# A decoder layer on one core: two groups overlapped in the opening, own rows for groups 2 and 3, 71 tiles, fewer idle products

## The reference

```python
x = x + self_attention(layernorm(x))             # 16 heads of 8, RoPE on q and k
x = x + cross_attention(layernorm(x), context)   # 77 context tokens
x = x + moe(layernorm(x))                        # 8 experts, hidden 512, gelu, top 2 of 8
# moe(x) = layer_norm(x + sum_k score_k * expert_k(x)) * gamma + beta
```

## Time and profile before

| | before |
|---|---|
| median of 3 runs | 628.62 us (627.22 to 629.9) |
| profiled execution | 631.22 us, of it span 629.4 us |
| mean granted clock of TensorE | 0.964 of 2.4 GHz |
| PE busy | 552.9 us (88%) |
| DVE busy | 388.3 us (62%) |
| ACT busy | 333.3 us (53%) |
| POOL busy | 344.0 us (55%) |
| DMA moved | 55.74 MB, mean 89 GB/s |

### The profile page before, as it was taken

One profiled execution on the slowest core, in us unless ns is written; L12 is line 12 of the kernel. 1 busy time (PEld: TensorE's weight loads), 2 busy tenths in 40 slices (PEclk: granted clock), 3 DMA queues, 4 the chain that ended last, 5 costly groups with the idle time before them and its releaser, 6 DMA issues.

```text
span 629.4 us, 22381 instructions
## 1 busy us (share of the span) xinstructions
PE 552.9 (88%) x7839; PEld 412.4 (66%) x7842; DVE 388.3 (62%) x1285; ACT 333.3 (53%) x866; POOL 344.0 (55%) x467
## 2 busy tenths in 40 slices
PE   4547899899999999999999999978999999999991
PEld 1224566556666666666666677758988999999630
DVE  2375867567677768766868656764556544444176
ACT  1112647456566566566666666553554555555143
POOL 4432738574344485484566627665765644444374
PEclk9696999899999999999999999997999999999997
DMA  4431232314147534044041313012223322222292
GB/s 105 145 116 35 63 104 74 97 36 146 49 130 211 160 104 127 19 118 118 17 117 33 88 43 107 25 57 61 73 78 86 91 62 64 57 54 61 78 248 87
DMA packets 74450, 55.74 MB, mean 89 GB/s; under 512 B 9040, under 2 KB 70997, under 8 KB 74354
## 3 DMA queue, kind: packets, MB, share of 16 engines
q1 hardware_dynamic: 68914, 45.40, 25.9%
q0 software_dynamic: 4384, 8.53, 4.1%
q10 hardware_dynamic: 1056, 0.52, 0.3%
HBM read 33.62 MB, written 19.23 MB: 84 GB/s over the span
## 4 chain that ended last, share of the span: by engine, by line
PE 57%; DVE 17%; issue 8%; DMA 6%; POOL 6%; ACT 3%; SPq 1%; POOLq 0%; DVEq 0%; ACTq 0%
PE S L980 8%; DVE nmp L1250 8%; PE AV L810 6%; PE W L854 5%; PE ST L778 5%; PE SM L1006 4%; PE AV L909 4%; PE AV L1006 4%; PE SM L835 3%; PE ST L784 3%; DMA ks<-routed 3%; DMA expert_out<-va,ks 2%; DVE onorm L1261 2%; PE S L746 1%; PE SM L823 1%
## 5 line engine op out<-in xcount | busy, mean ns | idle before, releaser
L1250 DVE TENSOR_REDUCE nmp<-S 128x4 bf16<-128x512 f32 (+1 forms) x256 | 142.4, 578 | 59.0 <-PE S L746 58.9
L1061 ACT ACTIVATE prob<-ST 128x512 f32<-128x512 f32 (+1 forms) x256 | 138.2, 591 | 70.0 <-PE ST L784 69.6
L1175 ACT ACTIVATE va<-S,b1s 128x128 f32<-128x128 f32 x288 | 82.1, 368 | 72.8 <-PE S L980 71.9
L1815 POOL DMA_INDIRECT expert_out<-va,ks x72 | 70.6, 981 | 65.2 <-DVE va L1562 56.6
L778 PE MATMUL ST<-nmt,onesr 32*77 32x128 bf16 (+1 forms) x1024 | 74.5, 220 | 15.5 <-DVE nmp L1250 12.2
L778 PEld LDWEIGHTS ST<-nmt,onesr 32*77 32x77 bf16 (+1 forms) x1024 | 53.8, 102 | 48.8 <-issue 43.9
L810 PE MATMUL AV<-prob,va 77*32 77x128 f32 (+1 forms) x2048 | 82.9, 280 | 0.0
L980 PE MATMUL S<-va 128*128 128x128 f32 x576 | 79.5, 282 | 2.7 <-DVE va L1549 1.5
L1749 POOL DMA_INDIRECT routed<-pay,dest x64 | 66.4, 1037 | 17.4 <-issue 16.2
L980 PEld LDWEIGHTS S<-va 128*128 128x128 f32 x576 | 72.2, 197 | 4.4 <-issue 3.6
L909 PE MATMUL AV<-onesr,idb 128*128 128x256 bf16 x435 | 68.3, 272 | 0.0
(11 more groups left out here) (236 smaller groups left out, 1152.4 us busy)
## 6 DMA issues: line engine op xcount, KB each, us to landing
ks<-routed SPq DMA_DIRECT2D x72, 65.0 KB, 1.9
qs<-q_parts SPq DMA_DIRECT2D x32, 128.0 KB
ks<-k_parts SPq DMA_DIRECT2D x32, 128.0 KB, 2.7
q2s<-q_parts SPq DMA_DIRECT2D x32, 128.0 KB
k2s<-k_parts SPq DMA_DIRECT2D x32, 77.0 KB
xin<-x SPq DMA_DIRECT2D x8, 256.0 KB, 3.1
q_parts<-rpart SPq DMA_DIRECT2D x8, 256.0 KB
k_parts<-rpart SPq DMA_DIRECT2D x8, 256.0 KB, 2.7
```

Source lines behind the costliest of these rows:

```text
L1061: act.activation(prob[0:st.keys, j, :], ST[j % 2][0:st.keys, :], ACT.Exp, scale=SCALE).then_inc(s_exp, 1)
L1175: last = act.activation(ht[:, (c + 1) % 4, q, :], S[k][:, q * P:(q + 1) * P], ACT.Gelu, bias=b1s[:, bass.ds(b + q, 1)])
L1250: V.tensor_reduce(nmp[:, st.at % 2, row_tile(p), 0:NB], S[p % 2][:, 0:NB * st.keys].rearrange("p (b k) -> p b k", b=NB), AX.X, ALU.max, ne ...
L1815: pool.indirect_dma_start(out=expert_out, out_offset=bass.IndirectOffsetOnAxis(ap=xr[:, at % ROUND, D + 1:D + 2].bitcast(U32), axis=0), in ...
```

## The change

- **Opening.** ACT issues the loads of the identity and of the q and k weights; SP loads x of both groups first. VectorE and POOL normalize groups 0 and 1 first; the normalized rows of group 1 go to space in `xn3all` and their transpose to `x2t`, so neither group waits for the other's buffer. `FIRST_ITEMS` mixes the two groups and puts both `v` last. For groups 0 and 1 VectorE adds (`turned`) in POOL's place. ACT issues two of the four spread DMAs of group 0's q and of its k. The bias rows move from VectorE to POOL, ACT copies their products out of PSUM. TensorE makes 12 products on the identity at the start, 12 instead of 16 idle products later, and 6 more after each pair of scores of steps 0 and 1.
- **Own rows.** q and k rows of groups 2 and 3 lie in the space of `w1s`; their spreads wait for no step, group 3's moves from step 8 to step 7; those of groups 4 and 5 wait for groups 0 and 1. SP waits at step 20 for the last step of group 3 before it loads `w1`.
- **Tiles.** 71 tiles are computed; 72 are still loaded.
- **Outputs carry the token's row.** The gates are doubled, each expert's output adds the token's row once, and the last norm takes 4 times the epsilon. `keep` and `tokens_of` go, and each of the eight sums has its own PSUM bank.
- **Idle products.** In a step with one of the eight projections the idle products ahead of the transposed maxima (L922) go, the others (L802) stay.

```diff
+TILES = (NTOK * TOPK) // P + E - 1
...
-            job(max(free, made + 3), "spread", g)
+            job(made + 2 if g == 3 else made + 3, "spread", g)
...
-        job(last + NORM, "keep", g)
...
-FIRST_ITEMS = [(name, g) for g in range(2) for name in ("xnt", "q", "rq", "k", "rk", "v")]
+FIRST_ITEMS = [("xnt", 0), ("q", 0), ("rq", 0), ("xnt", 1), ("k", 0), ("rk", 0),
+               ("q", 1), ("rq", 1), ("k", 1), ("rk", 1), ("v", 0), ("v", 1)]
...
+        FAR = (2, 3)
+        w1s = sb("w1s", [P, E * HID])
+        far_q, far_k = (w1s[:, k * NB * TOK:(k + 1) * NB * TOK].bitcast(F16).rearrange("p (n b t) -> p n b t", n=2, b=NB)
+                        for k in range(2))
...
-        SUM = (S[0], S[1], ST[0], ST[1])
+        SUM = (S[0], S[1], ST[0], ST[1], AV, SM, W[0], W[1])
...
-        WARM = 16
+        WARM = 12
...
+        MINE, OTHERS = (0, 1), (2, 3)
...
+                turn(NT // ROUND - 1, c, lambda k, c=c: NT - ROUND + c + k < TILES)
...
+        EARLY_WARM = 12
...
+            def own_before(g):
+                if g < GS:
+                    return None
+                return SELF_STEP[(g - (4 if g < 6 else 2)) * GS + GS - 1]
+            def cross_before(g):
+                return CROSS_STEP[(g - 2) * GS + GS - 1] if g >= 2 else None
...
+                spread("q", q_parts, rows_of(g)[0], g, True, own_before(g), MINE if g == 0 else range(4))
...
-            def keep(g):
...
+                if n == 20:
+                    for k in range(2):
+                        sp.wait_ge(s_st[k], NJ // 2 * (SELF_STEP[(FAR[-1] + 1) * GS - 1] + 1))
...
-            def idle_at(st):
-                own = [name for j in range(NJ) for name, g in items_at(st, j)]
-                return 3 if st.slot < SEQS or any(name in PROJECTIONS for name in own) else 6
+            def idle_at(st, m):
+                own = sum(name in PROJECTIONS for j in range(NJ) for name, g in items_at(st, j))
+                if own == 0:
+                    return 3 if st.slot < SEQS else 6
+                return (3, 0)[m]
...
+                    dense(idle_at(st, 1), AV[:, 2 * L:4 * L])
...
+            for _ in range(EARLY_WARM):
+                mm(SM[:, 0:P], idf[:, :], idf[:, :], start=True, stop=True)
             for name, g in FIRST_ITEMS:
                 work(name, g)
-            pe.wait_ge(s_const, 16 * len(CONSTS))
             pe.wait_ge(s_bvb, 2)
             mm(S[0][:, 0:D], bvb[:, 0, :], wself[:, 1, :], start=True, stop=True).then_inc(s_cbp, 1)
             mm(S[1][:, 0:D], bvb[:, 1, :], wcross[:, 1, :], start=True, stop=True).then_inc(s_cbp, 1)
             pe.wait_ge(s_set, SET_STEPS)
             dense(WARM, ST[0][:, :])
-            pe.wait_ge(s_cb, 2)
+            pe.wait_ge(s_cbm, 2)
             for st in STEPS[0:AHEAD]:
                 for m in range(2):
                     scores(st, m)
+                    dense(6, ST[1][:, :])
...
-            for k in range(2):
-                pe.wait_ge(s_keep[k], 16 * NG // 2)
...
-            def tokens_of(n):
...
-                mm(SUM[n % 4][:, :], idf[:, :], xn3all[:, n * FC * D:(n + 1) * FC * D], start=True, stop=False)
-            for n in range(4):
-                tokens_of(n)
-            pe.wait_ge(s_yw, NT)
+            pe.wait_ge(s_yw, TILES)
             dense(20, W[0][:, :])
             for n in range(CHUNKS):
...
+                    last = mm(SUM[n][:, :], idf[:, :], y2[n][:, k, :], start=(k == 0), stop=(k == TOPK - 1))
...
-                if 2 <= n and n + 2 < CHUNKS:
-                    tokens_of(n + 2)
...
+            act.dma_start(idf[:, :], ident).then_inc(s_idf, 16)
+            act.dma_start(wraw, w_self[:, 0:4, :]).then_inc(s_wraw, 16)
...
+            work("xnt", 0)
+            work("xnt", 1)
+            high_part(0, 0)
+            high_part(0, 1)
+            act.wait_ge(s_park["q"], 16)
+            spread_rows(act, "q", q_parts, rows_of(0)[0], True, OTHERS)
+            high_part(1, 0)
+            act.wait_ge(s_park["k"], 16)
+            spread_rows(act, "k", k_parts, rows_of(0)[1], False, OTHERS)
+            high_part(1, 1)
+            act.wait_ge(s_set, SET_STEPS)
+            work("v", 0)
+            work("v", 1)
+            act.wait_ge(s_cbp, 2)
+            for k in range(2):
+                move(cfull[:, k, :], S[k][:, 0:D], s_cbm)
...
-            def bias_rows():
...
+            def turned(g, k):
+                for name in (("q", "rq"), ("k", "rk"))[k]:
+                    bank, c = item(name, g)
+                    dve.wait_ge(s_wf[bank], c)
+                V.tensor_tensor(ra[:, k, :], ra[:, k, :], rb[:, k, :], ALU.add).then_inc(s_sum, 1)
...
-                did(V.tensor_scalar(gden[:, :], gexp[:, :], 1.0, None, ALU.add))
+                did(V.tensor_scalar(gden[:, :], gexp[:, :], 1.0, 0.5, ALU.add, ALU.mult))
...
             statistics(0)
+            statistics(1)
             normed_group(0)
+            normed_group(1)
+            statistics(2)
             dve.wait_ge(s_first, 16 * len(FIRST))
-            for name, g in FIRST_ITEMS:
-                if (name, g) == ("xnt", 1):
-                    statistics(1)
-                    normed_group(1)
-                work(name, g)
-            bias_rows()
+            for g in range(2):
+                for k, names in enumerate((("q", "rq"), ("k", "rk"))):
+                    for name in names:
+                        work(name, g)
+                    turned(g, k)
+            normed_group(2)
             dve.wait_ge(s_set, SET_STEPS)
-            statistics(2)
-            normed_group(2)
...
-                    V.tensor_scalar(yw[:, (c - 1) % 4, :], (AV, SM)[k][:, 0:D], xr[:, r, D:D + 1], None, ALU.mult).then_inc(s_yw, 1)
+                    V.scalar_tensor_tensor(yw[:, (c - 1) % 4, :], (AV, SM)[k][:, 0:D], xr[:, r, D:D + 1], xr[:, r, 0:D],
+                                           ALU.mult, ALU.add).then_inc(s_yw, 1)
...
+            def bias_values():
+                pool.wait_ge(s_const, 16 * len(CONSTS))
+                G.tensor_scalar(bvb[:, 0, :], idf[:, :], 0.0, bself[:, 4:5], ALU.mult, ALU.add).then_inc(s_bvb, 1)
+                G.tensor_scalar(bvb[:, 1, :], idf[:, :], 0.0, bcross[:, 2:3], ALU.mult, ALU.add).then_inc(s_bvb, 1)
...
+            def bias_rows():
...
+                pool.wait_ge(s_cbm, 2)
+                did(G.tensor_tensor(below[:, :], idf[:, 32:33], idf[:, 64:65], ALU.add))
+                did(G.tensor_tensor(cfull, cfull, cadd, ALU.add))
+                did(G.tensor_copy(c3[:, :, :], cfull))
+                for rest in (below[:, :], idf[:, 64:65]):
+                    did(G.tensor_scalar(cgone, c3[:, :, :], rest, None, ALU.mult))
+                    did(G.tensor_tensor(cfull, cfull, cgone, ALU.subtract))
+                    did(G.tensor_copy(c3[:, :, :], cfull))
...
-                        if st.i == 0:
-                            pool.wait_ge(s_keep[g % 2], 16 * (g // 2))
...
             set_up()
             norm_group(0)
+            norm_group(1)
+            set_up_more()
+            norm_group(2)
             for k in range(2):
-                turned(0, k)
                 low_part(0, k)
-            norm_group(1)
+            bias_values()
             for k in range(2):
-                turned(1, k)
                 low_part(1, k)
-            norm_group(2)
+            bias_rows()
```

More of the change, by code:

```diff
@@ L296, in decoder_layer, with normed_of, turned_of @@
         cfull = raw[:, 10:12, :]
+        cadd, cgone = raw[:, 6:8, :], raw[:, 8:10, :]
         xn3all = sb("xn3all", [P, SEQS * D])
         xn3t = sb("xn3t", [P, TOK])
+        def normed_of(g):
+            return xn3all[:, 0:TOK].rearrange("p (i d) -> p i d", i=GS) if g == 1 else xn1[:, :, :]
+        def turned_of(g):
+            return x2t if g == 1 else xnt
         pay = sb("pay", [P, 2, GS, TOPK, PAYW])
@@ L448, in near, with rows_of, spread_rows @@
             return STEPS[st.at + n] if 0 <= st.at + n < NS else None
+        def rows_of(g):
+            q, k = (far_q, far_k) if g in FAR else (qs, ks)
+            return q[:, g % 2, :, :], k[:, g % 2, :, :]
+        def spread_rows(eng, name, dram, rows, first, parts):
+            for c in parts:
+                h = c // 2 if first else c % 2
+                eng.dma_start(rows[c::4, :, :], dram[h].rearrange("(b i) n -> i b n", b=NB)).then_inc(s_rep[name], 16)
+        MINE, OTHERS = (0, 1), (2, 3)
         def wait_scattered(eng, g, seqs=range(GS)):
@@ L581, in park, with spread @@
                 sp.dma_start(dram.rearrange("h p n -> p h n"), parts).then_inc(s_park[name], 16)
-            def spread(name, dram, rows, g, first, last):
+            def spread(name, dram, rows, g, first, before=None, parts=range(4)):
                 sp.wait_ge(s_park[name], 16 * (g + 1))
-                if g >= 2:
+                if before is not None:
                     for k in range(2):
-                        sp.wait_ge(s_st[k], NJ // 2 * (last[(g - 2) * GS + GS - 1] + 1))
-                for c in range(4):
```

(27 more changed lines are left out.)

112 lines of the change are left out of this document (43 added, 69 removed).

## The result

The changed kernel takes 592.73 us as median (591.8 to 596.56) where the kernel before takes 628.17 beside it: a ratio of 0.945, 95% interval 0.941 to 0.949. The forecast was 591.5 in a range of 586 to 603. The profiled execution took 596.56, with a span of 594.7; before it was 631.2 and 629.4. So 34.7 us of span are to be found in the traces; the forecast had 37.1.

What follows compares the result with a forecast made beforehand. TensorE was taken to bound most of the run, then VectorE's maxima. Savings of 17.9 + 3.0 + 2.7 + 10.9 + 2.0 + 0.6 = 37.1 us off the median 628.6 gave 591.5 us, range 586 to 603.

Steps and rivals of the forecast that it cites:

- The opening: Before step 0: groups 0 and 1 normalized first, so step 0 starts at 32.6 instead of 50.52; minus 17.9 us.
- Steps 0 and 1: First two attention steps: projections, transposes, scores and value products at full instead of half clock; minus 3.0 us.
- Own rows: Near step 10: group 3's rows come earlier, so TensorE's DMA stall and the slow products after it go; minus 2.7 us.
- Idle products: Steps with a projection: TensorE alone sets the second half, so three idle products fewer save 0.33 each; minus 10.9 us.
- Start of the experts: Stretch from the last attention step to the first expert product: no gain forecast, 0.
- Tile 72: Expert stage: one turn fewer, at a period of 2.00 us; minus 2.0 us.
- The tail: Last sums: token products go, 2.3 us gained, but first two sums at half clock cost 1.7; net minus 0.6 us.
- B: Opening: clock does not rise, maxima rounds stretch, steps 0 and 1 stay slow; 603.5 us, chance 0.10.
- C: Opening: group 0's rows late, behind ACT's high part of group 1 and SP's 16 constants; up to 4 us, 595.5, chance 0.12.
- D: Steps with a projection: idle products were not on the path, removal only lengthens the wait for maxima; 602.4 us, chance 0.08.
- E: Projection steps: idle products had kept the clock full; without them it falls in each; slower, 664 us, chance 0.02.

Runs made afterwards that it cites:

- The last run: Kernel before, with only the idle products ahead of the turned maxima removed in steps with a projection: 620.37 us against 630.34, ratio 0.9825.

## Why the prediction was right, point by point

**The opening (17.9, measured 16.4).** The order was right in every link but the last, and the 1.5 us too much are in two landings. The k sum ended near 17.0 (worked out 16.7) and its low part at 18.94 (18.6). Then the parked rows took 2.8 us from issue to landing, where I took the median 2.1 of the earlier trace rows, and the last spread 4.2 instead of 2.7: the rows landed at about 26.6, and the first scores came at 26.73 instead of 25.0. In the forecast ScalarE's copies (24.9) ended last before the scores and the rows (24.4) just before them; the copies did end at 25.3, but the rows came after them. The four rounds took 7.4, worked out as 7.6. I used a median for two transfers out of a range whose upper ends, 5.4 and 4.1, stood in the same rows. The move of the sums to VectorE cost nothing on this path: group 0's two additions took 0.69 us each. Those of group 1, off the path, took 1.02 and 1.33, with POOL making a low part or bias values beside them.

**Steps 0 and 1 (3.0, and 0.3 for an idle group; measured 2.9).** Near, 0.4 less in sum, and the run without products in the rounds shows the same 2.7 from the other side.

**Own rows (2.7, measured 2.9 and 2.6).** Right in mechanism, and in size by the traces: the stall and the clock that falls after it come back together when the rows are shared again. The medians of that pair differ by 1.2 only.

**Idle products (10.9; measured 10.1, 10.5 and 10.7 in three pairs of traces).** The reading "a projection makes TensorE alone set the second half" holds in most of the 33 steps: 28 intervals between two steps are shorter by 0.33 (0.32 to 0.33), and five more by 0.05 to 0.27, for a reason that was not looked for. The same reading would have failed in the other half of the same steps, where the products are free by the trace.

**Start of the experts (0, measured 1.2).** A gain that I didn't see: the load of the first routed rows landed after 1.9 us instead of 3.06 (chain of the kernel before, then of the changed kernel):

```profile
422.03 3.06 DMA ks<-routed
```

```profile
390.12 1.90 DMA ks<-routed
```

Chance alone is unlikely. The last run is a second trace of a kernel with the keep DMAs, and by the updates of the load's semaphore it took 3.07 us there (issued 431.68, TensorE not yet waiting for it); in the twelve traces without them it took 1.8 to 2.4. But both slow loads have one more thing that no other has: a packet of the instruction queue q8 in flight beside the load's data (0.87 to 1.90 and 0.68 to 1.93 us after the issue). Which of the two is the cause stays open.

**Tile 72 (2.0, measured 2.1, and 1.9 by itself).** Right.

**The tail (0.6, measured -0.5).** The price of the clock was right to the tenth: 1.7, by the runs whose sums ran at full clock. Too large was the gain of 2.3. VectorE's waits of 1.48 and 0.46 us did go, 1.9 in all, but 1.0 came back at once. (No run takes this part of the change back; it is read from the two traces.) POOL's product with gamma takes 1.27 us. Before, the first of the two fell into VectorE's wait of 1.48 (timeline of POOL, the kernel before):

```profile
606.17 1.27 POOL L487 TENSOR_TENSOR xn3all<-xn3all,gammar 128x512 f32<-128x512 f32 x1
```

Now VectorE has work there, and its small scaling (L1634, else 0.17) ends with POOL's product; before, this happened at the second one alone. The slow sums cost the rest, 0.65 us before the first statistics and 1.0 before the second (timeline of VectorE and POOL, the changed kernel):

```profile
564.19 0.89 DVE L1629 BATCH_NORM_STATS2 xnt<-S 128x6 f32<-128x128 f32 x4 [10.30 <-PE S L1072]
...
566.94 0.89 DVE L1629 BATCH_NORM_STATS2 xnt<-S 128x6 f32<-128x128 f32 x4 [1.24 <-PE S L1072]
...
572.62 1.27 POOL L518 TENSOR_TENSOR xn3all<-xn3all,gammar 128x512 f32<-128x512 f32 x1
...
572.74 1.17 DVE L1634 TENSOR_SCALAR xnt<-xnt 128x4 f32<-128x4 f32 x1
```

The forecast priced the wait that went, and not what ran beside it. The Trainium skill, "SBUF — State Buffer", section "SBUF: two separate sides", says that VectorE and GpSimd share a pair of ports as an exclusive lock, which an operation of VectorE takes part in when it runs in a 2-port mode, or has two inputs in SBUF beside a GpSimd operation that reads SBUF; the one that comes second is blocked until the other is through. The scaling agrees with it, if it runs in such a mode, which no trace tells: it ends 0.02 us after POOL's product.

The Trainium skill, "TensorE: Matmul & The Clock Gate", section "HAM oscillation — how this bites in real kernels", lets the gate drop the clock in a wait for DMA. The traces agree in part: after waits of 2.97 to 3.32 us the first sums took 5.16 to 5.40 us in seven traces, and after waits of 2.95 to 3.35 us 3.70 in three.

**The rivals.** B was true of a kernel without the idle products in the rounds; with them it did not come. C was right that group 0's rows come late, by 1.7 us, but for neither of its reasons. SP parked q at 16.14 and k at 18.96, at once when POOL's low parts ended (16.11 and 18.94), so it was not held up by the constants; and ScalarE issued its k spreads with SP's (21.76 and 21.75). What was late is the landing. D and E are both true of the half of the step that the change does not touch: taking those products away as well gives nothing back, and costs 5.5 us, 4.6 of them seen as falls of the clock.

## What to carry to other kernels

An idle product is on the path only where its engine ends last in that half of the loop, so decide it half by half, from what the engine waits for next; the same product one half further on can be free and help to hold the clock. Before work is taken out in front of a wait for DMA, add up the idle time that it leaves, and price the work behind it at half clock; before a wait of VectorE is counted as gain, look at what POOL does in it. A chain of few transfers is bounded by their range, not by their median. And a gain that nobody forecast, as at the start of the experts, needs a second trace of either kernel before it is put down to the change.

## What the runs showed of the hardware that was not expected

- After the same idle time the clock falls in some executions and not in others. In front of the last sums (waits of 2.95 to 3.35 us, 20 idle products ahead) it fell in seven of ten traces; single falls, each of 0.7 to 1.35 us, turn up in steps in which the other traces have none (at the 24th, 14th and 32nd step in three kernels).
- The clock column of the windows shows 1.00 from 10 to 14 us in the run without early products, while the pair of projections took 3.78 us, against 1.98 at full clock. So early in an execution the durations are to be read, not the column.
- With four spreads issued by two queues the first scores follow 4.0 to 4.8 us after the last one begins (eleven traces), and with one queue after 2.9 (one trace): the time that the second queue saves in issuing is gone again when the rows have landed, by this one comparison.
- The same load of 65 KB took 3.06 and 3.07 us in the two traces of kernels with the keep DMAs, both times with a packet of the instruction queue beside it, and 1.8 to 2.4 us in the twelve others.
